# Edge stage: rows of local destinations as one-byte numbers, eight groups per transfer in two buffers

## The chip, the cores and the metric

The kernel runs on one core of one Trainium2 chip. The metric is the device time of one execution in microseconds (us), the median of several runs. TensorE is called PE, VectorE DVE, ScalarE ACT, GpSimd POOL and SyncE SP, as in the profile; PEld is PE's weight load, and SPq and POOLq are the sequencers of SP and POOL.

## What is computed

One graph attention layer over 6250 nodes and 206250 edges (100000 pairs in both directions and the self loops, sorted by destination), and behind it a mixture of 16 experts, of which each node uses two:

```
z  = layernorm(x) @ W                       # 4 heads of 64
e  = leaky_relu(es[src] + ed[dst], 0.01)    # es, ed: z against a_src, a_dst
ex = exp(e - max over the destination's edges)
x  = x + segment_sum(ex / denom[dst] * z[src], dst)
x  = x + moe(layernorm(x))                  # top 2 of 16 experts, layernorm behind it
```

The change is in the attention's edge part: for each edge the number of its destination within a tile of 128 nodes (the local destination, dst & 127) is wanted.

## The kernel before

The kernel has five stages. Stage A projects the nodes and writes a table of z with the source scores, 260 floats a row, to HBM (`z_table`). It also takes dst & 127 of all edges (L502), turns that into bf16 (L503, `dst_mod_h`) and stores it in HBM as one long row (`dst_rows`, L305). Stage B is the edge stage. Stages C, D and E route the nodes to experts, run these and combine their results.

Stage B works on 403 groups of 4 x 128 edges. A group whose edges belong to more than one tile of 128 destination nodes is visited once for each tile; the program has a fixed 451 visits, with tables (`visit_group`, `visit_word`, `group_free`) computed in stage A that say which group and tile a visit is. The loop is written out, and each engine has its own fixed order:

- POOL gathers. For each group it waits until the group four before it has been used (`group_free`, on `b_msg`) and issues four indirect DMAs (L681), each of 128 rows of `z_table`, into one of the four slots of `ring`. That makes 1612 gathers.
- SP relays. It waits for a group's four gathers and adds one to `b_group` (L629, `relay`), on which ACT waits. It also loads the local destinations: a transfer (L632) reads a piece of `dst_rows` and writes it to all 128 partitions of `dst_bc`, SP waits for its landing and adds one to `b_rows` (L643), on which DVE waits. A buffer is loaded again when DVE has made the last comparison on it (`b_ST`, L637 to L638 are that wait).
- DVE at step v: the sum of the scores for visit v - 5 (L747), the comparison ST (L734) for visit v, the leaky relu (L752), the accumulation of visit v - 8 (L835), the shift (L758), the comparison S (L740) for visit v - 6, the clamp (L765) and the message (L821) for visit v - 6, whose end frees the ring. ST compares the 512 local destinations of a group, the same in all partitions, with the partition's number (`iota_p`), and gives 128x512 floats, which are PE's weights for fetching destination scores (L927).
- PE at step v: four products (L927) for visit v and four (L938) for visit v - 6. All are f32 and are seen as eight weight loads and eight matmuls each.
- ACT: the copy of the source scores out of the ring (L866), the local destinations of L740 (L855) and the exponentials (L873, L875).

In the last 40 to 50 steps DVE, ACT and PE also finish the attention and normalise (L780 to L811, L885, L898, L950).

Before the change the transfer of L632 holds two groups (a pair) as bf16, in four buffers. SP's order for group g is: if g is even, wait for the landing of pair g/2 + 3 and tell DVE; wait for the landing of group g and tell ACT; if g is odd, wait for the comparison and issue the load of pair (g - 1)/2 + 4.

Of the kernel before, what the change touches and what calls it, by code (L numbers as in the profile page):

```python
# [27 lines left out]
F32 = mybir.dt.float32  # L28
I32 = mybir.dt.int32
BF16 = mybir.dt.bfloat16  # L30
ALU = mybir.AluOpType
ACT = mybir.ActivationFunctionType
AX = mybir.AxisListType

P = 128
G = 4
RING = 4
ROWS = 8
SLOPE = 0.01
EPS = 1e-5  # L40
LEVEL = 64.0
# [61 lines left out]
def early(item, depth):  # L103

    return isinstance(item, int) and item < depth


def gnn_moe_kernel(nc, E, x, x_turned, src_cols, dst_cols, dst_flat, dst_last, W, a_src, a_dst, gate_w, gate_b, w1, b1, w2, b2, gamma, beta, out):
    N, D = out.shape
    HEADS, DH = a_src.shape  # L110
    EXPERTS, _, F = w1.shape
    TOP = 2
    NT = -(-N // P)
# [5 lines left out]
    GROUPS = -(-CHUNKS // G)  # L119
# [4 lines left out]
    VISITS = FULL + NT  # L124
    BLOCKS = -(-CHUNKS // P)
# [4 lines left out]
    assert N * TOP // P > HEAD  # L130

    z_table = nc.dram_tensor("z_table", [NT * P, ROW], F32).ap()
    dst_rows = nc.dram_tensor("dst_rows", [BLOCKS * P * P], BF16).ap()
    norm_rows = nc.dram_tensor("norm_rows", [NT * P, D], F32).ap()

    pair_rows = nc.dram_tensor("pair_rows", [(TOP * NT + TILES) * P, D], F32).ap()
# [3 lines left out]
    def sem(name):  # L140
        return nc.alloc_semaphore(name=name)

    def sb(ctx, name, shape, dt=F32):
        return ctx.enter_context(nc.sbuf_tensor(name, shape, dt))
# [4 lines left out]
    def over(ap, shape):  # L149
        return ap.to_broadcast(shape)  # L150

    with whole:
# [32 lines left out]
        group_free = sb(graph, "group_free", [1, GROUPS + 1], I32)  # L185
# [5 lines left out]
        def bulk_rstd(step, stats, at, ready):  # L191

            a, b, m = ln_tmp[:, 0, at], ln_tmp[:, 1, at], mean[:, at]
            step(nc.vector.tensor_tensor(m, stats[:, at, 1], stats[:, at, 4], ALU.add))
            step(nc.vector.tensor_scalar(m, m, 0.5, None, ALU.mult))
            step(nc.vector.tensor_tensor(a, stats[:, at, 1], m, ALU.subtract))
            step(nc.vector.tensor_tensor(a, a, a, ALU.mult))
            step(nc.vector.tensor_tensor(b, stats[:, at, 2], stats[:, at, 5], ALU.add))
            nc.vector.scalar_tensor_tensor(out=a, in0=b, scalar=1.0 / D, in1=a, op0=ALU.mult, op1=ALU.add).then_inc(ready, 1)

# [31 lines left out]
        with ExitStack() as ctx:  # L232
# [1 line left out]
            dst_raw = sb(ctx, "dst_raw", [P, BLOCKS * P], I32)  # L234
            dst_i = sb(ctx, "dst_i", [P, BLOCKS * P], I32)
            dst_mod = sb(ctx, "dst_mod", [P, BLOCKS * P], I32)
            dst_mod_h = sb(ctx, "dst_mod_h", [P, BLOCKS * P], BF16)
            wcat = sb(ctx, "wcat", [P, KD, D + 2 * HEADS])
            centred = sb(ctx, "centred", [P, KD, D + 2 * HEADS])
            wprod = sb(ctx, "wprod", [P, 2, KD, D])  # L240
# [314 lines left out]
        b_over = sem("b_over"); b_go = sem("b_go")  # L555
        b_pstep = sem("b_pstep"); b_nodes = sem("b_nodes")
        b_group = sem("b_group")
        PAIRED, PAIRS = ROWS // 2, -(-GROUPS // 2)
        b_dst = [sem(f"b_dst{i}") for i in range(PAIRED)]; b_rows = sem("b_rows")
        b_S = sem("b_S"); b_ST = sem("b_ST")  # L560
        b_dest = sem("b_dest"); b_estep = sem("b_estep"); b_arg = sem("b_arg"); b_p = sem("b_p")
        b_msg = sem("b_msg"); b_sum = sem("b_sum"); b_acc = sem("b_acc"); b_es = sem("b_es")
# [28 lines left out]
        with ExitStack() as ctx:  # L591
# [6 lines left out]
            es_edge = sb(ctx, "es_edge", [P, 4, G, HEADS])  # L598
            S = sb(ctx, "S", [P, MR, G, P])
            ST = sb(ctx, "ST", [P, MR, G * P])  # L600
            dst_bc = sb(ctx, "dst_bc", [P, ROWS, G * P], BF16)
            earg = sb(ctx, "earg", [P, 4, 3, G * HEADS])
            msg = sb(ctx, "msg", [P, MR, G, ROW])
            psE = [ps(ctx, f"psEb{i}") for i in range(SR // BANKED)]
# [14 lines left out]
            @block.sync  # L619
            def _(sp):  # L620
                npass = sp.value_load(npass_i[0:1, 0:1], min_val=1, max_val=PASSES_MAX)
                with sp.Fori(0, npass) as k:
                    def uses(s):
                        return len(range(s, GROUPS, RING))

                    def relay(g, s, r):

                        sp.wait_ge(b_landed[s], 16 * G * (k * uses(s) + r + 1))
                        sp.nop().then_inc(b_group, 1)  # L629

                    def load_pair(g, at):
                        sp.dma_start(dst_bc[:, 2 * at:2 * at + 2, :].rearrange("p o f -> p (o f)"),  # L632
                                     over(dst_rows[bass.ds(g * (G * P), 2 * G * P)].unsqueeze(0), [P, 2 * G * P])).then_inc(b_dst[at], 16)

                    def replace_pair(g, at):

                        done = sp.value_load(group_free[0:1, g + 1 - ROWS + RING:g + 2 - ROWS + RING], min_val=1, max_val=VISITS)  # L637
                        sp.wait_ge(b_ST, done)  # L638
                        load_pair(g, at)

                    def relay_pair(at, r):
                        sp.wait_ge(b_dst[at], 16 * (r + 1))
                        sp.nop().then_inc(b_rows, 1)  # L643
                    for at in range(PAIRED):
                        load_pair(2 * at, at)
                    for at in range(PAIRED - 1):
                        relay_pair(at, 0)

                    for g in range(GROUPS):
                        pair = g // 2 + PAIRED - 1  # L650
                        if g % 2 == 0 and pair < PAIRS:
                            relay_pair(pair % PAIRED, pair // PAIRED)
                        relay(g, g % RING, g // RING)
                        if g % 2 and g // 2 + PAIRED < PAIRS:
                            replace_pair(g + ROWS - 1, g // 2 % PAIRED)

                    for at in range(PAIRED):
                        sp.wait_ge(b_dst[at], 16 * len(range(at, PAIRS, PAIRED)))
                    for done, total in ((b_group, GROUPS), (b_rows, PAIRS), (b_S, VISITS), (b_ST, VISITS), (b_dest, VISITS), (b_estep, 3 * VISITS),
                                        (b_arg, VISITS), (b_p, VISITS), (b_msg, VISITS + 1), (b_sum, VISITS), (b_acc, VISITS), (b_es, VISITS),  # L660
                                        (b_fstep, FIN_STEPS), (b_rden, NB), (b_scaled, NT), (b_added, NB), (b_stats, NT), (b_var, len(SPANS)),
                                        (b_root, len(SPANS)), (b_ready, len(SPANS)), (b_xn, NT), (b_xT_ps, NT), (b_xT, NT), (b_log_ps, NT), (b_log, NT),
                                        *((b_saved[i], 16 * len(range(i, NT, XN))) for i in range(XN)), (b_pstep, PASS_STEPS), (b_nodes, 1)):
                        sp.wait_ge(done, total)
                    sp.wait_ge(b_over, 4 * k + 4)
                    sp.sem_inc(apart, 1)
                    sp.sem_clear(range(b_pstep.num, b_saved[-1].num + 1))
                    sp.sem_inc(b_go, 1)
# [21 lines left out]
            def _(dve):  # L690
# [5 lines left out]
                with dve.Fori(0, npass) as k:  # L696
# [28 lines left out]
                    def make_ST(v, s, r):  # L725
                        if early(v, SOON):
                            group = dve.value_load(visit_group[0:1, v:v + 1], min_val=0, max_val=GROUPS - 1)
                        else:
                            group = (word[0] >> (RING * TILE_SPAN).bit_length() - 1).with_bounds(min_val=0, max_val=GROUPS - 1)
                        slot = group & (ROWS - 1)  # L730
                        dve.wait_ge(b_rows, (group >> 1) + 1)
                        if not early(v, MR):
                            dve.wait_ge(b_dest, v - MR + 1)
                        nc.vector.tensor_scalar(ST[:, s % MR, :], dst_bc[:, bass.ds(slot, 1), :].rearrange("p o f -> p (o f)"), iota_p[:, 0:1], None, ALU.is_equal).then_inc(b_ST, 1)  # L734
# [91 lines left out]
                    def accumulate(v, s, r):  # L826
# [5 lines left out]
                        if not early(v, 1):  # L832
                            dve.wait_ge(b_acc, v)
                        at = acc[:, bass.ds(tile, 1), :].rearrange("p o c -> p (o c)")
                        nc.vector.tensor_tensor(at, at, psM[s % 2][:, 0:ROW], ALU.add).then_inc(b_acc, 1)  # L835
                    written_out(VISITS, SR, [(look_up, AHEAD + 1), (e_add, AHEAD), (make_ST, 0), (e_lrelu, AHEAD),
                                                       (accumulate, AHEAD + 1 + MSG_TO_ACC), (e_shift, AHEAD), (one_hot, AHEAD + 1),
                                                       (e_clamp, AHEAD), (message, AHEAD + 1), (finish, None)], steps=FINISH)
# [134 lines left out]
        with ExitStack() as ctx:  # L973
# [6 lines left out]
            total = sb(ctx, "total", [P, EXPERTS, NT])  # L980
# [7 lines left out]
            slot_i = sb(ctx, "slot_i", [P, 3, NT], I32)  # L988
            iota_h = sb(ctx, "iota_h", [P, P], BF16)
            tile_h = sb(ctx, "tile_h", [P, NT], BF16)  # L990
            HALF = (NT + 1) // 2
            LR = 3
            THIRD = -(-NT // 3)
            low = sb(ctx, "low", [P, LR, THIRD, P], BF16)
            high = sb(ctx, "high", [P, LR, THIRD, 3, TILES], BF16)
# [469 lines left out]
```

## Time and profile before

| | us |
|---|---|
| median of 3 runs, without the profiler | 2771.41 |
| lowest and highest of them | 2768.65, 2774.7 |
| span of the profiled execution | 3426.8 |
| of it, ahead of the first gather of stage B | 79.36 |
| of it, from the first to the end of the last gather | 2724.53 |
| of it, behind that | 622.91 |

The profiled execution is 655 us longer than the median of the others. Engines' busy times are shares of its span: PE 68%, POOL 54%, DVE 49%, ACT 22%. Durations of single instructions can be read from it as they are; its waits must be read with care, for the reason the prediction gives.

### The profile page before, as it was taken

Reading aid. Unit: us, or ns where it says so; the run is one execution under the profiler, and the core shown is the slowest. Engines: PE = TensorE matmul, PEld = TensorE weight load, DVE = VectorE, ACT = ScalarE, POOL = GpSimd, SP = SyncE. Lnnn points to the kernel's source line nnn. Section 1 sums busy time; section 2 is a strip of 40 time slices with the busy share of each in tenths; the row PEclk is TensorE's granted clock in tenths of the full one; section 3 lists DMA queues with packets and bytes.
Section 4 is the critical chain, followed back from the end, with each engine's and each line's share of the span. In section 5 each row is a group of like instructions: output and inputs, shape, how many; then the busy total and the mean of one; then the engine's idle time right before and its main releaser. Section 6 shows DMA issues by size and latency. Waiting matters only on the chain. (4 is left out here: it accounts for less than half of the span.)

```text
span 3426.8 us, 54564 instructions
## 1 busy us (share of the span) xinstructions
PE 2313.2 (68%) x10829; PEld 1980.6 (58%) x10830; DVE 1684.5 (49%) x4860; ACT 753.9 (22%) x2906; POOL 1837.6 (54%) x1951
## 2 busy tenths in 40 slices
PE   6556666566667576666666665656567774899997
PEld 4545555455556565555555554545456662699995
DVE  6544445444455444454544454545456666533335
ACT  4111111111111111111111111111114442455556
POOL 1655555555555565555555555555555531555556
PEclk9677777776777666777777777777776775899999
DMA  8333333333334333333333333333334430563337
GB/s 285 97 102 96 105 92 99 98 103 93 101 101 105 97 106 100 97 100 103 97 100 97 103 101 105 94 100 97 100 99 109 111 88 21 184 185 105 106 104 234
DMA packets 183059, 378.55 MB, mean 110 GB/s; under 512 B 38773, under 2 KB 86816, under 8 KB 182410
## 3 DMA queue, kind: packets, MB, share of 16 engines
q0 software_dynamic: 87744, 243.02, 26.5%
q1 hardware_dynamic: 72152, 111.89, 10.4%
q10 hardware_dynamic: 22898, 20.85, 2.3%
q14 instruction: 189, 1.55, 0.2%
q8 instruction: 76, 1.25, 0.1%
HBM read 341.68 MB, written 33.93 MB: 110 GB/s over the span
## 5 line engine op out<-in xcount | busy, mean ns | idle before, releaser
L681 POOL DMA_INDIRECT ring<-z_table,src_idx x1612 | 1543.3, 957 | 1186.6 <-DVE msg L821 677.8
L938 PE MATMUL psMb<-msg,S 128*128 128x260 f32 x3608 | 1269.1, 512 | 515.1 <-DVE msg L821 413.0
L938 PEld LDWEIGHTS psMb<-msg,S 128*128 128x128 f32 x3608 | 878.7, 256 | 693.2 <-DVE msg L821 425.9
L927 PEld LDWEIGHTS psEb<-nodes,ST 128*128 128x128 f32 x3608 | 612.3, 241 | 515.5 <-issue 475.2
L927 PE MATMUL psEb<-nodes,ST 128*128 x3608 | 558.0, 279 | 451.3 <-DVE earg L765 183.2
L835 DVE TENSOR_TENSOR acc<-acc,psMb 128x260 f32 x451 | 190.3, 422 | 1080.3 <-remote 820.6
L821 DVE TENSOR_TENSOR msg<-ring,psPb 128x1024 f32<-128x1024 f32 x451 | 546.5, 1212 | 8.1 <-issue 8.1
L866 ACT COPY es_edge<-ring 128x16 f32 x451 | 91.8, 204 | 1128.5 <-issue 1045.0
L873 ACT ACTIVATE msg<-earg 128x16 f32<-128x16 f32 x451 | 95.2, 211 | 1064.9 <-DVE earg L765 927.3
L740 DVE TENSOR_TENSOR S<-iota_f,psPb 128x512 f32<-128x512 f32 x451 | 306.4, 679 | 2.7 <-issue 2.7
L734 DVE TENSOR_SCALAR ST<-dst_bc,iota_p 128x512 f32 x451 | 221.5, 491 | 53.7 <-issue 49.7
L1237 PE MATMUL psHd<-xT,w_sb 128*128 128x128 f32 x1728 | 213.2, 277 | 0.0
L1249 PE MATMUL psYd<-w_all,hid 128*128 x864 | 204.3, 380 | 1.7 <-ACT hid L1272 1.7
L1237 PEld LDWEIGHTS psHd<-xT,w_sb 128*128 128x128 f32 x1728 | 204.3, 194 | 0.1
L1205 POOL DMA_INDIRECT rows_sb<-norm_rows,src_sb x108 | 111.0, 1028 | 168.9 <-DVE src_sb L1282 151.5
L747 DVE TENSOR_TENSOR earg<-es_edge,psEb 128x16 f32<-128x16 f32 x451 | 73.8, 164 | 219.7 <-issue 105.1
L1293 DVE COPY xT<-psXd 128x256 f32<-128x256 f32 x108 | 45.8, 424 | 264.1 <-PE psXd L1227 257.9
L1249 PEld LDWEIGHTS psYd<-w_all,hid 128*128 128x128 f32 x864 | 156.0, 191 | 18.6 <-issue 1.9
L1260 ACT COPY w_sb<-w_all 128x1024 f32 x108 | 112.8, 1045 | 162.2 <-PE psHd L1237 85.6
L1212 POOL DMA_INDIRECT pair_rows<-y_sb,dst_sb x108 | 106.7, 988 | 45.6 <-issue 36.1
L1272 ACT ACTIVATE hid<-psHd,b1T 128x128 f32<-128x128 f32 x432 | 123.2, 368 | 30.9 <-issue 26.2
L855 ACT ACTIVATE psPb<-dst_col,visit_base 128x4 f32 x451 | 120.4, 267 | 42.4 <-DVE msg L821 20.5
(202 smaller groups left out, 1445.5 us busy)
## 6 DMA issues: line engine op xcount, KB each, us to landing
dst_bc<-dst_rows SPq DMA_DIRECT2D x202, 256.0 KB
ring<-z_table,src_idx POOLq DMA_INDIRECT x1612
w_all<-in_L_ffn_w_dram SPq DMA_DIRECT2D x32, 512.0 KB
b_sb<-in_L_ffn_b_dram ACTq DMA_DIRECT2D x108, 128.0 KB
got<-pair_rows SPq DMA_DIRECT2D x48, 256.0 KB, 4.5
z_table<-z_out SPq DMA_DIRECT2D x49, 130.0 KB, 7.1
norm_rows<-xnb ACTq DMA_DIRECT2D x49, 128.0 KB
acc<-in_x_turned_dram SPq DMA_DIRECT2D x12, 512.0 KB, 8.9
```

The costliest lines, as they stand in the source:

```text
L681: nc.gpsimd.indirect_dma_start(ring[:, s, c, :], None, z_table, bass.IndirectOffsetOnAxis(ap=at, axis=0)).then_inc(b_landed[s], 16)
L734: nc.vector.tensor_scalar(ST[:, s % MR, :], dst_bc[:, bass.ds(slot, 1), :].rearrange("p o f -> p (o f)"), iota_p[:, 0:1], None, ALU.is_equ ...
L740: nc.vector.tensor_tensor(S[:, s % MR, :, :], over(iota_f[:, 0:P].unsqueeze(1), [P, G, P]), over(psP[s % 2][:, G * HEADS:G * HEADS + G].un ...
L821: nc.vector.tensor_tensor(msg[:, s % MR, :, 0:D].rearrange("p g (h d) -> p g h d", h=HEADS), ring[:, bass.ds(slot, 1), :, 0:D].rearrange(" ...
L835: nc.vector.tensor_tensor(at, at, psM[s % 2][:, 0:ROW], ALU.add).then_inc(b_acc, 1)
L855: nc.scalar.activation(psP[s % 2][:, G * HEADS:G * HEADS + G], dst_col[:, bass.ds(group * G, G)], ACT.Identity, bias=visit_base[:, v:v + 1])
L927: last = nc.tensor.matmul(dest_of(s)[:, c * SH:(c + 1) * SH], ST[:, s % MR, c * P:(c + 1) * P], nodes[:, bass.ds(tile, 1), :].rearrange("p ...
L938: last = nc.tensor.matmul(psM[s % 2][:, 0:ROW], S[:, s % MR, c, :], msg[:, s % MR, c, :], start=c == 0, stop=c == G - 1)
L1237: last = nc.tensor.matmul(psH[s % 2][:, f * P:(f + 1) * P], w1_sb[:, s % 2, c, f * P:(f + 1) * P], xT[:, s % 2, c, :], start=c == 0, stop= ...
L1249: last = nc.tensor.matmul(psY[s % 2][:, 0:D], hid[:, s % 2, f, :], w2_f, start=f == 0, stop=f == FC - 1)
L1260: nc.scalar.copy(w1_sb[:, s % 2, :, :].rearrange("p c f -> p (c f)"), w_all[:, bass.ds(e, 1), 0:KD * F].rearrange("p o f -> p (o f)")).the ...
L1272: last = nc.scalar.activation(hid[:, s % 2, f, :], psH[s % 2][:, f * P:(f + 1) * P], ACT.Relu, bias=b1T[:, bass.ds(e, 1), f:f + 1].rearran ...
```

## The change

`dst_rows`, `dst_mod_h` and `dst_bc` become unsigned one-byte numbers in place of bf16. `dst_bc` holds 16 groups in place of 8, in the same number of bytes, as two buffers of eight groups. One transfer loads eight groups (4096 bytes to each partition) in place of two (2048 bytes). There are 51 transfers in place of 202. SP waits for the landing of part g // 8 + 1 ahead of group g with g % 8 = 2, three groups after the load was issued (behind group g with g % 8 = 7), where before it waited in the next group. DVE waits on `b_rows` with the group's number divided by 8. The comparison of L734 reads bytes.

```diff
-ROWS = 8
+ROWS = 16
+LOADED = 8
-    dst_rows = nc.dram_tensor("dst_rows", [BLOCKS * P * P], BF16).ap()
+    dst_rows = nc.dram_tensor("dst_rows", [BLOCKS * P * P], U8).ap()
-            dst_mod_h = sb(ctx, "dst_mod_h", [P, BLOCKS * P], BF16)
+            dst_mod_h = sb(ctx, "dst_mod_h", [P, BLOCKS * P], U8)
-            dst_bc = sb(ctx, "dst_bc", [P, ROWS, G * P], BF16)
+            dst_bc = sb(ctx, "dst_bc", [P, ROWS, G * P], U8)
-                    def load_pair(g, at):
-                        sp.dma_start(dst_bc[:, 2 * at:2 * at + 2, :].rearrange("p o f -> p (o f)"),
-                                     over(dst_rows[bass.ds(g * (G * P), 2 * G * P)].unsqueeze(0), [P, 2 * G * P])).then_inc(b_dst[at], 16)
+                    def load_rows_of(part, at):
+                        sp.dma_start(dst_bc[:, LOADED * at:LOADED * (at + 1), :].rearrange("p o f -> p (o f)"),
+                                     over(dst_rows[bass.ds(part * (LOADED * G * P), LOADED * G * P)].unsqueeze(0), [P, LOADED * G * P])).then_inc(b_dst[at], 16)
-                    for at in range(PAIRED):
-                        load_pair(2 * at, at)
-                    for at in range(PAIRED - 1):
-                        relay_pair(at, 0)
+                    for part in range(PARTED):
+                        load_rows_of(part, part)
+                    for part in range(PARTED):
+                        relay_rows_of(part)
                     for g in range(GROUPS):
-                        pair = g // 2 + PAIRED - 1
-                        if g % 2 == 0 and pair < PAIRS:
-                            relay_pair(pair % PAIRED, pair // PAIRED)
+                        part = (g + LOADED - 2) // LOADED
+                        if g % LOADED == 2 and PARTED <= part < PARTS:
+                            relay_rows_of(part)
                         relay(g, g % RING, g // RING)
-                        if g % 2 and g // 2 + PAIRED < PAIRS:
-                            replace_pair(g + ROWS - 1, g // 2 % PAIRED)
+                        if g % LOADED == LOADED - 1 and g // LOADED + PARTED < PARTS:
+                            replace_rows_of(g // LOADED + PARTED, g // LOADED % PARTED)
-                        dve.wait_ge(b_rows, (group >> 1) + 1)
+                        dve.wait_ge(b_rows, (group >> (LOADED.bit_length() - 1)) + 1)
```

## Rows read from the trace of the kernel before

**Rows 1.** The page: busy time by engine, and PE's granted clock in slices of 86 us.
```profile
PE 2313.2 (68%) x10829; PEld 1980.6 (58%) x10830; DVE 1684.5 (49%) x4860; ACT 753.9 (22%) x2906; POOL 1837.6 (54%) x1951
...
PEclk9677777776777666777777777777776775899999
```

**Rows 2.** Stretches: us; PE, PEld, DVE, ACT, POOL busy; PEclk; DMA share; GB/s.
```profile
0.00:79.36 79.36, 54.68 (x206) 41.11 (x207) 47.30 (x176) 38.51 (x105) 5.20 (x19) 0.99 0.87 294
79.36:2803.89 2724.53, 1729.87 (x7349) 1480.45 (x7350) 1362.89 (x3769) 393.41 (x2037) 1543.25 (x1612) 0.72 0.38 101
2803.89:3426.80 622.91, 528.64 (x3275) 459.08 (x3273) 274.26 (x917) 322.03 (x765) 289.11 (x320) 0.89 0.42 131
```

**Rows 3.** Lines: the gathers; count, busy us, mean ns, idle before and its releasers.
```profile
L681 POOL DMA_INDIRECT ring<-z_table,src_idx x1612 | 1543.3, 957 | 1186.6 <-DVE msg L821 677.8 <-issue 503.5 <-DVEq L696 5.3
```

**Rows 4.** Waits: engine, line, whom for, us in total, times, longest.
```profile
DVE acc L835 <- remote: 820.6, 112, 11.9
```

**Rows 5.** Timeline, start of the edge stage: start us, us, engine, line, operation.
```profile
79.36 1.44 POOL L681 DMA_INDIRECT ring<-z_table,src_idx  x1 [5.34 <-DVEq L696]
81.10 3.99 POOL L681 DMA_INDIRECT ring<-z_table,src_idx  x1 [0.30 <-issue]
92.05 3.03 POOL L681 DMA_INDIRECT ring<-z_table,src_idx  x1 [0.30 <-issue]
80.83 13.43 DVE L718 TENSOR_TENSOR acc<-acc,decided 128x3136 f32<-128x3136 f32 x4
```

**Rows 6.** Timeline: one comparison ST and the gather beside it.
```profile
286.95 0.49 DVE L734 TENSOR_SCALAR ST<-dst_bc,iota_p 128x512 f32 x1 [0.27 <-issue]
287.10 1.16 POOL L681 DMA_INDIRECT ring<-z_table,src_idx  x1 [0.30 <-issue]
```

**Rows 7.** Timeline of a stall and of the visits behind it.
```profile
1499.78 0.60 PE L938 MATMUL psMb<-msg,S 128*128 128x260 f32 x2
1510.10 0.42 DVE L835 TENSOR_TENSOR acc<-acc,psMb 128x260 f32 x1 [9.24 <-remote]
1512.41 0.48 DVE L734 TENSOR_SCALAR ST<-dst_bc,iota_p 128x512 f32 x1
1515.19 0.48 DVE L734 TENSOR_SCALAR ST<-dst_bc,iota_p 128x512 f32 x1
1516.09 1.71 PE L927 MATMUL psEb<-nodes,ST 128*128 x8
1517.66 3.58 PE L938 MATMUL psMb<-msg,S 128*128 128x260 f32 x8
1521.07 0.95 PE L927 MATMUL psEb<-nodes,ST 128*128 x8
1521.88 2.00 PE L938 MATMUL psMb<-msg,S 128*128 128x260 f32 x8
```

**Rows 8.** DMA queues from 300 to 2500 us: packets, MB, share of 16 engines; issues.
```profile
q0 software_dynamic: 62659, 173.84, 30.4%
q1 hardware_dynamic: 23475, 42.74, 6.5%
...
dst_bc<-dst_rows SPq DMA_DIRECT2D x163, 256.0 KB
```

**Rows 9.** Waits of SP's queue.
```profile
SPq L643 <- DMA dst_bc<-dst_rows: 150.2, 56, 3.4
SPq L309 <- DMA dst_rows<-dst_mod_h: 1.5, 1, 1.5
```

**Rows 10.** Lines of DVE by shape: count, busy us, mean ns, idle before.
```profile
L821 DVE TENSOR_TENSOR msg<-ring,psPb 128x1024 f32<-128x1024 f32 x451 | 546.5, 1212 | 8.1 <-issue 8.1
L740 DVE TENSOR_TENSOR S<-iota_f,psPb 128x512 f32<-128x512 f32 x451 | 306.4, 679 | 2.7 <-issue 2.7
L503 DVE CAST dst_mod_h<-dst_mod 128x1664 bf16<-128x1664 int32 x1 | 1.0, 1026 | 0.0
```

**Rows 11.** The tile ring: shortest, median and longest gather, ns.
```profile
L681 POOL DMA_INDIRECT ring<-z_table,src_idx x1612: 940/946/3989, 79.4 to 2802.9; - x180
```

More of the change, by code:

```diff
@@ L30 @@
 BF16 = mybir.dt.bfloat16
+U8 = mybir.dt.uint8
 ALU = mybir.AluOpType
@@ L557, in gnn_moe_kernel @@
         b_group = sem("b_group")
-        PAIRED, PAIRS = ROWS // 2, -(-GROUPS // 2)
-        b_dst = [sem(f"b_dst{i}") for i in range(PAIRED)]; b_rows = sem("b_rows")
+        PARTED, PARTS = ROWS // LOADED, -(-GROUPS // LOADED)
+        assert PARTS * LOADED * G <= BLOCKS * P
+        b_dst = [sem(f"b_dst{i}") for i in range(PARTED)]; b_rows = sem("b_rows")
         b_S = sem("b_S"); b_ST = sem("b_ST")
@@ L629, in relay @@
                         sp.nop().then_inc(b_group, 1)
-                    def load_pair(g, at):
-                        sp.dma_start(dst_bc[:, 2 * at:2 * at + 2, :].rearrange("p o f -> p (o f)"),
-                                     over(dst_rows[bass.ds(g * (G * P), 2 * G * P)].unsqueeze(0), [P, 2 * G * P])).then_inc(b_dst[at], 16)
-                    def replace_pair(g, at):
-                        done = sp.value_load(group_free[0:1, g + 1 - ROWS + RING:g + 2 - ROWS + RING], min_val=1, max_val=VISITS)
+                    def load_rows_of(part, at):
+                        sp.dma_start(dst_bc[:, LOADED * at:LOADED * (at + 1), :].rearrange("p o f -> p (o f)"),
+                                     over(dst_rows[bass.ds(part * (LOADED * G * P), LOADED * G * P)].unsqueeze(0), [P, LOADED * G * P])).then_inc(b_dst[at], 16)
@@ L638, in replace_pair, with replace_rows_of, relay_rows_of @@
+                    def replace_rows_of(part, at):
+                        freed = (part - PARTED + 1) * LOADED - 1 + RING
+                        done = sp.value_load(group_free[0:1, freed:freed + 1], min_val=1, max_val=VISITS)
                         sp.wait_ge(b_ST, done)
-                        load_pair(g, at)
-                    def relay_pair(at, r):
-                        sp.wait_ge(b_dst[at], 16 * (r + 1))
+                        load_rows_of(part, at)
+                    def relay_rows_of(part):
+                        sp.wait_ge(b_dst[part % PARTED], 16 * (part // PARTED + 1))
@@ L653, in _ @@
                         relay(g, g % RING, g // RING)
-                        if g % 2 and g // 2 + PAIRED < PAIRS:
-                            replace_pair(g + ROWS - 1, g // 2 % PAIRED)
-                    for at in range(PAIRED):
-                        sp.wait_ge(b_dst[at], 16 * len(range(at, PAIRS, PAIRED)))
-                    for done, total in ((b_group, GROUPS), (b_rows, PAIRS), (b_S, VISITS), (b_ST, VISITS), (b_dest, VISITS), (b_estep, 3 * VISITS),
+                        if g % LOADED == LOADED - 1 and g // LOADED + PARTED < PARTS:
+                            replace_rows_of(g // LOADED + PARTED, g // LOADED % PARTED)
@@ L660, in _ @@
+                    for at in range(PARTED):
+                        sp.wait_ge(b_dst[at], 16 * len(range(at, PARTS, PARTED)))
+                    for done, total in ((b_group, GROUPS), (b_rows, PARTS), (b_S, VISITS), (b_ST, VISITS), (b_dest, VISITS), (b_estep, 3 * VISITS),
                                         (b_arg, VISITS), (b_p, VISITS), (b_msg, VISITS + 1), (b_sum, VISITS), (b_acc, VISITS), (b_es, VISITS),
```

## The prediction
> **What bounds the kernel now.** I read the page first. POOL is busy 54% of the span and PE 68%, and the granted clock of PE is 0.6 to 0.7 in the slices of the edge stage against 0.9 at both ends [rows 1]. No engine looks full, so the next view is the three stretches around the gathers: 79.36 us ahead of the first, 2724.53 us with them, 622.91 us behind the last [rows 2]. Only the middle one holds what the change touches, apart from one conversion and one store.
>
> In the middle stretch the gathers are the plainest clockwork. 1612 of them take 957 ns each, and POOL is idle 1186.6 us before them [rows 3]. That idle time has two parts: 503.5 us of "issue" and 677.8 us of waiting for a message of DVE [rows 3]. Single gathers show what most of the first part is: 0.30 us before each [rows 5, 6]. So a gather that waits for nothing costs 0.957 + 0.30 = 1.257 us, and all of them 1543.3 + 1612 x 0.30 = 1543.3 + 483.6 = **2026.9 us**. What is left of the stretch, 2724.5 - 2026.9 = 697.6 us, is POOL waiting for the ring.
>
> Now the profiled execution against the runs. It spans 3426.8 us where the median is 2771.4. Take the same head and tail: 2771.4 - 79.4 - 622.9 = 2069.1 us would be left for the gathers, 42 us above their own 2026.9. So without the profiler nearly all of the 697.6 us of waiting is gone, and POOL's issuing sets the stage's pace: 2069.1 / 451 visits = 4.6 us a visit. (If something lies around the span in the median, the 42 shrink by it.) What the waits of the profiled execution are is seen in the largest group of DVE: 820.6 us before the accumulation, 112 times, put down to no engine here [rows 4]. One such place: PE's last product of the visit ends at 1500.38, and the accumulation that wants it starts at 1510.10 [rows 7]. Every engine then stands, and the ring runs dry. That is a disturbance the timed runs don't pay, at least not at this size; I take no gain or loss from it.
>
> How far the others are from POOL's 4.6 us a visit: DVE, when nothing holds it, starts its comparisons 2.78 us apart (1512.41 and 1515.19). PE needs 0.95 + 2.00 = 2.95 us a visit at the upper clock, but 1.71 + 3.58 = 5.29 us at the lower [rows 7]. Stretches at the lower clock, and the last 40 to 50 steps where DVE, PE and ACT have more to do, are my guess for the 42 us.
>
> **The change part by part.**
>
> *The transfers.* 202 of 256 KB become 51 of 512 KB (4096 bytes to each of 128 partitions), so the bytes written fall from 53 to 27 MB. From 300 to 2500 us SP's queue takes 6.5% of the 16 engines, POOL's 30.4% [rows 8]: 36.9% together, so the engines are not the bound, and halving 6.5% frees about 3% of something with 60% to spare. Price: 0. Cover: the ring. It lets POOL run four groups ahead, so a landing may come late by what the loop leaves: three groups of 5.03 us (15.1 us) from the end of a group's gathers until its slot is wanted again, less the landing, SP's and ACT's relay, and two steps of DVE (2 x 2.78) with a message of 1.2 us. With 2 us for the landing that is about 15.1 - 2 - 0.5 - 5.6 - 1.2 = 5.8 us of slack. The landing time and the relay are my estimates, from the transfers' longest wait of 3.4 us [rows 9] as an upper end of the landing.
>
> *The larger burst.* It puts 128 packets of 4096 bytes in front of a gather's packets where there were 128 of 2048. Now 6.5% of 2200 us is 143 us on each engine for 163 transfers, 0.9 us each [rows 8]. If the time grows with the bytes, a burst takes 1.8 us on each engine where it took 0.9. Bounds for the extra delay of a gather in front of which it falls: 0 and 0.9 us, below the 5.8 us of slack. Price 0; the upper bound without that cover is 51 x 0.9 = 46 us.
>
> *SP's order.* Before, SP stood 150.2 us for landings of pairs, 56 times, at most 3.4 us [rows 9], right ahead of the relay of a group. A group lands 5.03 us after the one before, so a wait of 3.4 us behind one relay ends before the next is due; it hid nothing and delayed nothing. After the change the landing is asked for only three groups (15 us) after the load and the wait is nothing. The waits on the comparison stay satisfied: when group g has landed, DVE has sent the message of group g - 4, and it compares six visits ahead of its messages. Saved on SP: 150 us, 151 issues and 151 waits; on the path: 0. Bounds: 0 and, if each of the 202 waits had held a relay and the ring had no slack, the 42 us that POOL waits at all.
>
> *DVE's wait on the rows.* It now asks for whole parts of eight groups. The part of groups 8m + 8 and up is told ahead of the relay of group 8m + 2, and DVE reaches the comparison of group 8m + 8 only behind the sum for 8m + 3 or later, which needs a later relay. So this wait is never last. At the start two transfers of 512 KB stand in for four of 256 KB (three of them waited for). DVE's first comparison comes behind 13.43 us of L718, which end at 94.26 us [rows 5], and this hides a few us. Price 0.
>
> *The comparison on bytes.* L734 takes 0.48 to 0.49 us for 512 elements [rows 6, 7]. Two-source operations show the plain rate: (1212 - 679) / 512 = 1.04 ns an element [rows 10], by which 512 elements alone are 533 ns, more than all of L734. So L734 runs in a faster mode, about twice the plain rate. So does the conversion of int32 to bf16: 1664 elements in 1.03 us, 1.73 at the plain rate [rows 10]. Widths of four and two bytes are thus seen in this mode; one byte is not. I take the same duration (nearest rows), price 0. The other end is the plain rate: 0.48 + 256 x 1.04 ns = 0.75 us, 0.27 us more a visit, 120 us of DVE time in all, hidden by 4.6 - 2.8 = 1.8 us a visit of DVE's slack, except at the end of the stage.
>
> At the other end there would also be a gain. A gather that starts 0.15 us after such a comparison takes 1.16 us [rows 6] where the median is 0.946 [rows 11]; another takes 3.03 us beside L718 [rows 5]. The mean of 957 ns is 11 above the median of 946 [rows 3, 11]: 1612 x 0.011 = 17.7 us, of which the first five (1.44, 3.99 and three of about 3.03, [rows 5]) are 14.5 - 5 x 0.95 = 9.8 too long. So about **8 us** go to the comparisons, and would come back if L734 left the fast mode.
>
> The Trainium skill (SBUF — State Buffer, "Who interferes with whom") says the same of the cause: VectorE in a two-port mode and GpSimd exclude each other from a shared pair of ports for a whole instruction. The Trainium skill (Vector Engine (DVE) Microarchitecture Reference, 5.1 Performance modes) gives this mode's conditions without a width of the elements; by that rule the bytes keep the mode and the sum stays at 0, and no row here has a one-byte operand to test it. The Trainium skill (DMA: Bandwidth & Descriptors, Rules for kernel authors) asks for transfers of 1 MiB and more. By it the change is a gain for DMA time; what it would be here is 0, since the share of 6.5% [rows 8] binds nothing.
>
> *Stage A.* The conversion writes bytes (1.0 us, or 1.0 more at the plain rate, beside the projection) and the store is half as large. SP waits 1.5 us for it [rows 9], at the end of the stage; half the bytes might give 0.2 us. Price 0, bounds -0.3 and +1.
>
> **Sum.** Against the profiled execution: 0 of 3426.8 us. Against the median: 2771.4 + 0 = **2771 us**.
>
> **The rivals.**
>
> *The bytes drop the comparison to the plain rate, and POOL gains.* For it: no one-byte operand is in the trace. Against it: four and two bytes behave alike. It gives 2771 - 8 = 2763 us.
>
> *The relays held the ring.* SP's 150 us in front of relays mattered in the undisturbed execution too, or lighter DMA traffic speeds landings. Against it: 3.4 us at most within 5 us. It can take from the 42 us only; a third of them gives 2771 - 14 = 2757 us.
>
> *Slower: the plain rate meets the end of the stage.* In the last 49 visits DVE also finishes the attention. If DVE is the bound there, each visit grows by 0.27 us, 13 us in all, less 1 us that POOL gets back there. That gives 2783 us. It decides once the comparison is longer and DVE is the last to be ready; if the comparison on bytes took over 0.48 + 1.8 = 2.3 us it would decide in every visit. The larger burst in a place without slack would end in the same range (up to 46 us, and a third of that is 15).
>
> *The change does not do what it says* (DMA splits rows of 4096 bytes otherwise, or reads the same bytes of HBM more slowly): it ends where the forecast does, since SP has 15 us for the landing.
>
> **How the numbers follow.** No change, within 0.2% (5.5 us, about what a measurement of this kernel can tell from none): 0.60. The first rival 0.12 and the second 0.11, both faster; the third and the burst 0.17, slower. The forecast's own range is 2766 to 2777. For 8 in 10 the range reaches into both sides: below through 2757 to 2750, above through 2783 to 2788.
>
> **What would show it.** Right: L734 at 0.48 us, gathers still 0.95 + 0.30 us apart, 26 MB less on SP's queue, and L643's wait near 0, with the runs unchanged. Wrong: L734 near 0.75 us (first or third rival, told apart by the sum of POOL's idle time behind 2560 us); a mean gather below 0.95 us; or waits for rows before L734. What would make the whole prediction wrong is a wrong reading of the 655 us: if the stalls were partly paid in the timed runs, the ring would have no slack there, and landings, relays and DVE's order would all count.

## The result, and the profile after

| | before | after |
|---|---|---|
| median of 12 runs, us | 2776.37 | 2786.62 |
| lowest, us | 2768.65 | 2783.12 |
| ratio, 95% interval | | 1.0039 (1.0029 to 1.0049) |

The change makes the kernel 0.4% slower, some 10 us. The forecast was no change, 2771 us. One of the 12 runs of the kernel before took 2913.96 us and is not in the ratio. Of the 15 us between the forecast and the measured 2786.62, 5 us are the kernel before itself, whose median was 2771.41 with 3 runs and is 2776.37 with 12.

The trace ahead of the prediction, 3426.8 us long, does not belong to the times beside it. Experiments e3 to e6 met a chip on which every kernel took 3409 to 3461 us, with or without the profiler (but for one run of 3684.97), and their traces show the stalls of [rows 4, 7]. So the first trace was very likely taken on a chip of that sort; its chip is not on record, and only one such chip was met, so a lasting property of it can't be told from a passing state. The changed kernel's trace is of the usual sort. So it is set beside a second trace of the kernel before (run e0 below), not beside [rows 2, 3].

The page of the changed kernel (first lines and granted clock) and its three stretches, with the columns of [rows 2]:

```profile
span 2783.2 us, 53814 instructions
PE 2253.5 (81%) x10829; PEld 1873.0 (67%) x10830; DVE 1709.0 (61%) x4860; ACT 720.6 (26%) x2906; POOL 1859.3 (67%) x1951
...
PEclk9676888788787877888688788888777669999998
```
```profile
0.00:79.30 79.30, 55.22 (x206) 41.52 (x207) 47.21 (x176) 38.55 (x105) 5.20 (x20) 0.93 0.86 292
79.30:2167.15 2087.85, 1675.41 (x7362) 1378.26 (x7363) 1388.46 (x3776) 361.93 (x2047) 1566.12 (x1612) 0.80 0.43 119
2167.15:2783.20 616.05, 522.85 (x3263) 453.18 (x3261) 273.31 (x911) 320.13 (x755) 287.98 (x320) 0.90 0.42 132
```

Its groups of gathers and of the comparison ST, which answer to [rows 3] and to L734 in [rows 6, 7]:

```profile
L685 POOL DMA_INDIRECT ring<-z_table,src_idx x1612 | 1566.1, 972 | 526.7 <-issue 444.7 <-DVE msg L825 77.0 <-DVEq L700 5.0
L738 DVE TENSOR_SCALAR ST<-dst_bc,iota_p 128x512 f32 x451 | 230.0, 510 | 98.0 <-issue 93.4 <-PE psEb L931 4.3
```

And SP's waits in the edge stage, its queue from 300 to 1900 us and its transfers, which answer to [rows 8, 9]:

```profile
SPq L632 <- DMA ring<-z_table,src_idx: 1994.3, 401, 11.6
SPq L647 <- DMA dst_bc<-dst_rows: 4.3, 2, 3.2
```
```profile
q1 hardware_dynamic: 5616, 20.45, 3.4%
...
dst_bc<-dst_rows SPq DMA_DIRECT2D x39, 512.0 KB, 4.0
```

The reader is to see that the change did on SP and on the DMA engines what it says. SP waits 4.3 us for rows, and its queue takes 3.4%. DVE's comparison is no longer than before. Yet the gathers take 972 ns each, where [rows 3] has 957 and the second trace of the kernel before, shown next, has 965.

### The profile page after: what moved, and what is told of

Its sections match the earlier page's. It is cut to its first block and busy times, and to the rows that moved or that the text cites. A ratio compares the mean times of both kernels' runs of the same rounds, so it can differ in the third digit from the quotient of the medians.

```text
span 2783.2 us, 53814 instructions
## 1 busy us (share of the span) xinstructions
PE 2253.5 (81%) x10829; PEld 1873.0 (67%) x10830; DVE 1709.0 (61%) x4860; ACT 720.6 (26%) x2906; POOL 1859.3 (67%) x1951
## 5 line engine op out<-in xcount | busy, mean ns | idle before, releaser
L685 POOL DMA_INDIRECT ring<-z_table,src_idx x1612 | 1566.1, 972 | 526.7 <-issue 444.7
L942 PE MATMUL psMb<-msg,S 128*128 128x260 f32 x3608 | 1199.2, 490 | 169.5 <-DVE msg L825 168.2
L942 PEld LDWEIGHTS psMb<-msg,S 128*128 128x128 f32 x3608 | 827.4, 241 | 334.2 <-DVE msg L825 186.6
L931 PEld LDWEIGHTS psEb<-nodes,ST 128*128 128x128 f32 x3608 | 548.9, 226 | 346.3 <-issue 323.3
L931 PE MATMUL psEb<-nodes,ST 128*128 x3608 | 535.1, 276 | 219.4 <-DVE ST L738 111.5
L738 DVE TENSOR_SCALAR ST<-dst_bc,iota_p 128x512 f32 x451 | 230.0, 510 | 98.0 <-issue 93.4
```

Source lines behind the costliest of these rows:

```text
L685: nc.gpsimd.indirect_dma_start(ring[:, s, c, :], None, z_table, bass.IndirectOffsetOnAxis(ap=at, axis=0)).then_inc(b_landed[s], 16)
L931: last = nc.tensor.matmul(dest_of(s)[:, c * SH:(c + 1) * SH], ST[:, s % MR, c * P:(c + 1) * P], nodes[:, bass.ds(tile, 1), :].rearrange("p ...
L942: last = nc.tensor.matmul(psM[s % 2][:, 0:ROW], S[:, s % MR, c, :], msg[:, s % MR, c, :], start=c == 0, stop=c == G - 1)
```

## The experiments

**The kernel before once more**, for a trace of the usual sort of chip; no edit.

> The kernel before, unchanged, for a trace without the stalls of the first. The changed kernel's trace has, from the first to the last gather, 2087.8 us: 1612 gathers at 0.946 + 0.305 us, 9.8 us of slow gathers at the start, 31 us because 138 later gathers take 1.1 to 1.2 us beside a comparison (L738), and 31 us of waits for the ring from group 374 on. Theory A (the collisions decide): this trace has the same end and fewer collisions, some 10 us less of them and fewer than 100 long gathers. Theory B (the end decides): the same collisions, 31 us, and about 20 us of waits at the end in place of 31. Theory C (the start or the tail): both sums equal, and the difference lies before 79 us or behind the last gather.

Its profiled run took 2773.76 us. Stretches, gathers, comparison and SP's waits:

```profile
0.00:79.06 79.06, 54.39 (x206) 41.01 (x207) 47.33 (x176) 38.56 (x105) 5.20 (x20) 0.98 0.88 295
79.06:2154.95 2075.89, 1671.83 (x7353) 1378.36 (x7354) 1388.88 (x3772) 361.48 (x2045) 1555.58 (x1612) 0.80 0.49 132
2154.95:2771.80 616.85, 524.69 (x3271) 455.95 (x3269) 273.93 (x913) 320.71 (x757) 288.12 (x320) 0.90 0.41 132
```
```profile
L681 POOL DMA_INDIRECT ring<-z_table,src_idx x1612 | 1555.6, 965 | 526.0 <-issue 453.9 <-DVE msg L821 66.4 <-DVEq L696 5.7
L734 DVE TENSOR_SCALAR ST<-dst_bc,iota_p 128x512 f32 x451 | 231.5, 513 | 99.0 <-issue 96.6 <-PE psEb L927 1.9 <-SPq L643 0.3
```
```profile
SPq L629 <- DMA ring<-z_table,src_idx: 1216.5, 403, 11.7
SPq L643 <- DMA dst_bc<-dst_rows: 623.7, 197, 4.4
```

The head and the tail are the same within 1 us. The middle stretch is 2087.85 - 2075.89 = 12.0 us longer after the change. POOL's own time is 1566.1 - 1555.6 = 10.5 us of that, its idle time 0.7 us. So the loss is in the duration of gathers, as theory A of the expectation above has it (its count of fewer than 100 long gathers was missed by one). From the starts and durations of all gathers (the first five left out, which stand beside L718 in both; a pause of POOL is 0.305 us where nothing is waited for, and a wait is what lies above that):

```
                                    before   after
gathers over 1.0 us                    100     138
what gathers take over 0.946 us, us   20.9    31.4
waits of POOL over 0.35 us, us        29.5    31.0
```

Where the long ones are, the timeline of the changed kernel shows (POOL, the copy of the scores on ACT, the comparison on DVE):

```profile
1116.48 0.20 ACT L870 COPY es_edge<-ring 128x16 f32 x1 [4.15 <-SPq L632]
1117.16 0.49 DVE L738 TENSOR_SCALAR ST<-dst_bc,iota_p 128x512 f32 x1 [0.27 <-issue]
1117.27 1.19 POOL L685 DMA_INDIRECT ring<-z_table,src_idx  x1 [0.30 <-issue]
...
1126.97 0.20 ACT L870 COPY es_edge<-ring 128x16 f32 x1 [4.69 <-SPq L632]
1127.65 0.53 DVE L738 TENSOR_SCALAR ST<-dst_bc,iota_p 128x512 f32 x1 [0.27 <-issue]
1127.72 0.95 POOL L685 DMA_INDIRECT ring<-z_table,src_idx  x1 [0.30 <-issue]
```

The comparison follows the copy by 0.68 us each time. At 1117 it starts 0.11 us ahead of a gather, and the gather takes 1.19 us. At 1127 it starts 0.07 us ahead, and the gather takes 0.95. Over the comparisons of both traces that start up to 0.40 us ahead of a gather:

```
ahead of the gather by, us   0-0.05  0.05-0.10  0.10-0.15  0.15-0.20  0.20-0.25  0.25-0.30  0.30-0.35  0.35-0.40
before: times                    34         95         42         11          3         15          3          5
before: gather longer by, us   0.00       0.02       0.24       0.19       0.12       0.09       0.04       0.00
after: times                     30        132         75         17          5          6          5          8
after: gather longer by, us    0.00       0.04       0.24       0.19       0.12       0.09       0.03       0.00
```

The cost of a collision is the same for bf16 and for bytes. What differs is how often the comparison falls into the window of 0.10 to 0.35 us: 74 times before, 108 times after. Gathers with a comparison that started up to 0.5 us ahead of them lose 16.0 us before and 27.2 us after, 11.2 us more; all others lose 4.9 and 4.3. So this one sort of collision is the whole difference of 10.5 us.

The comparison falls into the window by a rhythm. POOL starts a gather every 1.251 us. A group lands some 3.0 us behind the start of its fourth gather when nothing holds it up (in the changed kernel half of the odd groups reach ACT between 2.97 and 3.03 us behind it). SP, ACT and DVE pass that on in a fixed time. So the comparison meets the third gather of the next group at nearly the same distance, 0.07 us ahead in the median of these groups, just short of the window. A group that lands late misses the third gather. In the kernel before, that is so for most of the even groups, whose gathers are in flight beside the pair's transfer that SP issues one group earlier. An odd group, the late even group behind it, and the next odd group:

```profile
1110.64 0.20 ACT L866 COPY es_edge<-ring 128x16 f32 x1 [4.22 <-SPq L629]
1111.08 10.65 SPq L632 DMA_DIRECT2D dst_bc<-dst_rows  x2
1111.33 0.49 DVE L734 TENSOR_SCALAR ST<-dst_bc,iota_p 128x512 f32 x1 [0.28 <-issue]
1111.49 1.15 POOL L681 DMA_INDIRECT ring<-z_table,src_idx  x1 [0.30 <-issue]
...
1117.23 0.20 ACT L866 COPY es_edge<-ring 128x16 f32 x1 [5.99 <-SPq L629]
1117.91 0.49 DVE L734 TENSOR_SCALAR ST<-dst_bc,iota_p 128x512 f32 x1 [0.28 <-issue]
1117.94 0.95 POOL L681 DMA_INDIRECT ring<-z_table,src_idx  x1 [0.30 <-issue]
...
1120.99 0.20 ACT L866 COPY es_edge<-ring 128x16 f32 x1 [3.16 <-SPq L629]
1121.67 0.49 DVE L734 TENSOR_SCALAR ST<-dst_bc,iota_p 128x512 f32 x1 [0.28 <-issue]
1121.69 0.95 POOL L681 DMA_INDIRECT ring<-z_table,src_idx  x1 [0.30 <-issue]
```

The row of L632 holds two issues, at 1111.08 and 10.3 us later. The copy at 1110.64 is 2.9 us behind its group's fourth gather, and the comparison behind it strikes a third gather (1111.49). The copy at 1117.23 is 4.3 us behind its own; its comparison comes only when the third gather is over, starts 0.03 us ahead of the fourth and costs it nothing. SP's own wait for the pair is not what comes late here: it ended 0.36 us or more, in the median 1.21 us, ahead of each even group's relay.

By the same reckoning over groups 16 to 369 (median time from the start of a group's fourth gather to the copy on ACT, and how often the third gather of the next group took over 1.0 us):

```
                         even groups          odd groups
before                   3.30 us, 12 times    3.00 us, 37 times
bytes, pairs (e1)        3.05 us, 31 times    3.00 us, 37 times
after                    3.02 us, 50 times    2.99 us, 48 times
after + copies (e8)      3.59 us,  4 times    3.01 us, 54 times
```

**Theory A** in full: the change takes away the transfers that made every second group land 0.3 us late, and with them an accident that kept its comparison off the gather. The later runs test that. It covers the even groups, 38 of the 49 third gathers that the change adds. The odd groups add 11 with no change in their landing that the table can show; their comparison starts 0.06 us ahead of the gather before and 0.07 us after, close to the window's edge, and why those 11 were added stays open.

**Bytes alone**: U8 for `dst_rows`, `dst_mod_h` and `dst_bc`, and nothing else.

```diff
-    dst_rows = nc.dram_tensor("dst_rows", [BLOCKS * P * P], BF16).ap()
+    dst_rows = nc.dram_tensor("dst_rows", [BLOCKS * P * P], U8).ap()
```

> Bytes alone: the row is stored and compared as one-byte numbers, still two groups to a transfer in four buffers, with the order of SP as before. If the bytes make the loss (the comparison's hold on POOL, or its own length), the ratio to the kernel before is 1.004, as for the whole change. If the loss comes from eight groups to a transfer and from SP's new order, it is 1.000.

Measured: 1.0022 (1.0012 to 1.0033), between the two. A pair of bytes has half the bytes of a pair of bf16, and its even groups land 0.05 us late in place of 0.30 (table). In its one trace the long gathers sum to 21.7 us, only 0.8 more than before, and its profiled run (2776.96 us) is the second fastest of its 11; the ratio is the better witness. So by the ratios the loss comes in about two halves, with the bytes and with the eight groups. That the first half also comes by late landings is a reading of the table (31 third gathers in place of 12), not shown apart.

**Larger transfers alone**: bf16, ROWS = 8, LOADED = 4, SP's wait moved to the next group.

```diff
-                        part = (g + LOADED - 2) // LOADED
-                        if g % LOADED == 2 and PARTED <= part < PARTS:
+                        part = g // LOADED + 1
+                        if g % LOADED == 0 and PARTED <= part < PARTS:
```

> Larger transfers alone: bf16 as before, four groups to a transfer in two buffers, so that each transfer writes 4096 bytes to each partition as in the change, and there are 101 of them. SP waits for the landing in the next group, as before. If the burst of 512 KB is the cause, twice as many of them as in the change give a ratio of 1.004 to 1.008. If the bytes are the cause, it is 1.000. If it is that SP hardly waits between relays, it lies between 1.000 and 1.004, as SP here waits for every fourth group in place of every second.

Measured: 1.0059 (1.0043 to 1.0075), in the range that was expected if the burst of 512 KB is the cause. It doesn't tell that, for another cost came in. Two buffers of four groups leave no time between the last comparison on one and the first on the next, and DVE waits for the rows, a wait that neither the kernel before nor the changed one has:

```profile
DVE ST L738 <- SPq L647: 164.9, 48, 4.7
```

Its edge stage is 2090.5 us, 14.6 more than in e0. Of that POOL's waits are 11.3 us (40.8 in place of 29.5), its gathers 3.2. So most of its loss is waiting that the changed kernel (31.0 us of waits) doesn't have. A cost of the larger burst is bounded by e7 and e10 below, not by this run.

**The comparison one place later, idle copies on HBM, idle copies on ACT**: all on a chip where the kernel before took 3428.72 us (median of 23 runs).

```diff
-  [(look_up, AHEAD + 1), (e_add, AHEAD), (make_ST, 0), (e_lrelu, AHEAD),     # e3 (after), e4 (before)
+  [(look_up, AHEAD + 1), (e_add, AHEAD), (e_lrelu, AHEAD), (make_ST, 0),
```
```diff
+                        if g % 2 == 0 and g:                                  # e5
+                            sp.wait_ge(b_dst[PARTED], 16 * (g // 2))
                         relay(g, g % RING, g // RING)
+                        if g % 2 and g < GROUPS - 1:
+                            sp.dma_start(idle[g // 2 % 2, :, :],
+                                         over(dst_rows[bass.ds(2048 * (g % 64), 2048)].unsqueeze(0), [P, 2048])).then_inc(b_dst[PARTED], 16)
```
```diff
+                        for i in range(2):                                    # e6
+                            nc.scalar.copy(late[:, s % 4, i, :], ring[:, bass.ds(slot, 1), 0, 0:16].rearrange("p o c -> p (o c)"))
                         nc.scalar.copy(es_edge[:, s % 4, :, :],
```

> The changed kernel with DVE's comparison ST one place later in the visit, behind the leaky relu (L756 before L738); nothing is left out. In the trace of the changed kernel the comparison starts 0.88 us behind the relay of a group and so 0.1 to 0.2 us ahead of the third gather of the next group, which then takes 1.1 to 1.2 us. Theory A (the loss is these collisions): it now starts some 0.3 us later, just behind the gather's start; the 138 long gathers fall below 50, 15 to 30 us are saved, and the time is 2755 to 2770 us, below both kernels (ratio to before 0.993 to 0.999). Rival (the large transfers delay landings): nothing about them is changed, and the ratio stays at 1.004.

> The kernel before with the same move of the comparison behind the leaky relu. Theory A: its 80 or so collisions (20.8 us) go too, and it ends within 3 us of the changed kernel with the move, since nothing else of the change counts: ratio 0.993 to 0.999. Rival: if bytes and eight groups to a transfer cost time by themselves, this one stays 8 to 12 us below the changed kernel with the move.

> The changed kernel with extra work: behind every second group SP also copies 2048 bytes 128 times from HBM to HBM, into an array that nobody reads, and waits for it in the next group, as the kernel before did with its pairs. Theory A (the pairs' transfers made every second group land 0.3 us later, and so its comparison missed the gather): even groups land some 0.2 to 0.4 us later again, collisions fall from 31 to about 20 us, and the kernel with more work is 4 to 12 us faster than the changed one: ratio to before 0.999 to 1.002. Rival (DMA traffic costs time): it is slower than the changed kernel, ratio 1.004 to 1.010.

> The changed kernel with two copies of 16 elements on ACT, read by nobody, ahead of the copy of the source scores (L870), so that DVE's step starts some 0.2 to 0.3 us later behind each relay. Theory A: a longer path to DVE makes it faster, for the comparison starts behind the gather's start: collisions below 15 us, ratio to before 0.995 to 1.000. Rival (what counts is how soon DVE gets its scores): the delay can only cost, ratio 1.004 or more.

Measured: e3 1.0071 (1.0048 to 1.0094), e4 1.0085 (1.0058 to 1.0112), e5 1.0019 (0.9994 to 1.0043), e6 1.0007 (0.9983 to 1.0031). Of what theory A forecast, the ratios of e3, e4 and e6 were missed; the ratio of e5 lies in its range, with an interval that reaches up to the rival's, and the collisions of e6 fell below 15 us as forecast. The changed kernel was not run on this chip, and the first trace, of such a chip, has only 8.5 us of long gathers, so there was little to gain. The waits of e6:

```profile
DVE acc L840 <- remote: 801.7, 114, 11.7
POOL ring L686 <- DVE msg L826: 702.0, 172, 9.2
```

These are the stalls of [rows 4] and [rows 3], in a kernel whose timed runs took 3430 us. What e6 saves on gathers (3.7 us against the first trace) POOL stands idle longer (5.1 us).

The losses of e3 and e4 are collisions too. The gathers of e3:

```profile
L685 POOL DMA_INDIRECT ring<-z_table,src_idx x1612 | 1564.9, 971 | 1188.6 <-DVE msg L825 733.1 <-issue 450.5 <-DVEq L700 5.0
```

Its long gathers take 30.2 us and those of e4 31.1, where the first trace has 8.5; the idle time of POOL is within 3 us of that of [rows 3], and the stage is 24.0 and 20.4 us longer than there. Some 17.7 and 17.5 us of it are in gathers that end a wait for the ring. In the first trace the last comparison starts 0.79 us ahead of such a gather in the median, outside the window; one place later it starts 0.23 us ahead, inside it (137 and 130 times). So the same move that was to take the comparison out of the window put it in at another gather.

The idle copies of e6 did shift the comparison: where no stall comes between, it starts 1.08 us behind SP's relay in place of 0.88, and the long gathers are 4.9 us. Three of the kernels were run once more on another chip.

**The same on a chip of the usual sort** (before: 2776.8 us, 15 runs), with the kernel before under the idle copies of e6 as the fourth.

> The same kernel as e6_after_scores_late (two idle copies on ACT ahead of L870), since on the chip of that call every kernel, the one before too, took 3430 us, and POOL waited 693 us for the ring whatever the comparison did. Its trace there had the comparison 1.08 us behind the relay in place of 0.88, and 4.8 us of collisions in place of 31. On a chip where the kernel before takes some 2775 us, theory A says 31 - 5 = 26 us less than the changed kernel: ratio to before 0.994 (0.991 to 0.998). Rival (a later step of DVE costs as much as it saves): 1.002 to 1.006.

> The same kernel as e5_after_idle_copies, again for a chip where the kernel before takes some 2775 us. Theory A (a transfer behind every second group makes the next land late and its comparison miss the gather): even groups are relayed 3.0 us or more behind their fourth gather in place of 2.8, their collisions fall to a third, and the kernel with more work is faster than the changed one: ratio to before 0.999 to 1.002. Rival (DMA traffic costs time): 1.004 to 1.010.

> The same kernel as e3_after_later_compare, for a chip where the kernel before takes some 2775 us. The comparison came 1.09 us behind the relay there, as with the idle copies. Theory A: the same gain as with the idle copies, ratio 0.994 (0.991 to 0.998), without extra work. Rival: 1.004.

> The kernel before with the same two idle copies on ACT. Theory A, if collisions are all that tells the two kernels apart: it gains what it has of them in its own trace (20.8 us) less 5, and ends at ratio 0.994 as the changed kernel with the copies does, within 0.001. Rival (bytes or large transfers cost or save time of their own): the two differ by 0.002 or more.

```
                                          ratio to before (95%)      long gathers, us   edge stage, us
e7   after, two idle copies on ACT        0.9952 (0.9938 to 0.9965)        9.9              2063.5
e9   after, comparison one place later    0.9961 (0.9946 to 0.9976)       14.1              2067.9
e10  before, two idle copies on ACT       0.9959 (0.9946 to 0.9973)       13.6              2069.9
e8   after, idle copies on HBM            1.0009 (0.9996 to 1.0021)       30.4              2091.0
     after (first result)                 1.0039 (1.0029 to 1.0049)       31.4              2087.8
```

Long gathers and edge stage are of the one trace of each. The changed kernel's own ratio is from the first comparison, on other runs of the kernel before (median 2776.37); it was not run again beside e7 to e10.

The gathers of e7, and one of its groups:

```profile
L686 POOL DMA_INDIRECT ring<-z_table,src_idx x1612 | 1544.6, 958 | 524.0 <-issue 465.8 <-DVE msg L826 53.1 <-DVEq L701 5.1
```
```profile
1105.78 0.31 ACT L872 COPY late<-ring 128x16 f32 x2 [4.00 <-SPq L633]
1106.18 0.20 ACT L873 COPY es_edge<-ring 128x16 f32 x1
1106.55 0.94 POOL L686 DMA_INDIRECT ring<-z_table,src_idx  x1 [0.30 <-issue]
1106.87 0.49 DVE L739 TENSOR_SCALAR ST<-dst_bc,iota_p 128x512 f32 x1 [0.27 <-issue]
```

Work that nobody reads, put on the path to DVE, takes the changed kernel from 1.0039 to 0.9952, 24 us, inside theory A's range. The comparison now starts behind the gather's start, and 21.5 of 31.4 us of long gathers are gone; the stage is 24.3 us shorter. The move of the comparison (e9) gives nearly the same with no extra work. With the idle copies the kernel before (e10) and the changed one (e7) differ by 0.0007, inside both intervals: once collisions are few, bytes and eight groups cost and save nothing that can be measured. Nothing here supports a cost of theirs apart from the rhythm. The expectation of e10 was met in that difference and missed in size: 0.9959 in place of 0.994, with 13.6 us of long gathers left in place of 5.

e8 is the reverse test: it adds 201 copies of 256 KB to the changed kernel, in the place where the pairs' transfers were, twice the 51 transfers' bytes. Its ratio is 1.0009, some 8 us below the changed kernel, in theory A's range and below the rival's. Its even groups strike a third gather 4 times in place of 50. But its profiled run was the slowest of its 11 (2786.3 us against a median of 2778.2), with more collisions of first gathers (28 in place of 14) and a median gather of 949 ns in place of 946, so its sum of 30.4 us and its stage of 2091.0 us don't show the gain that the median does. The link from late landings to the time thus rests on the ratio and on the even groups' count, not on a trace that adds up.

## Why the prediction was wrong

*POOL's issuing sets the pace*: right. The middle stretch was put at 2069.1 us and is 2075.9, 49.0 us above the 2026.9 of gathers and pauses. What I called 42 us of waiting is 29.5 us of waits, nearly all from group 374 on, 12.3 us of longer gathers (1555.6 in place of 1543.3) and 7 us of pauses, which are 0.305 us and not 0.30.

*The 655 us are a disturbance that the timed runs don't pay*: right for the runs shown, wrong in the cause. I took the profiler for it; on the chip of e3 to e6 the timed runs pay it too.

*The transfers, SP's order, DVE's wait on the rows, stage A*, each at 0: as far as the ring and SP are concerned, right. SP's waiting for rows fell from 623.7 to 4.3 us (I had 150.2 from the other chip [rows 9]), 26.4 MB left its queue, POOL's long waits went from 29.5 to 31.0 us, and head and tail stayed.

*The comparison on bytes*, same duration: right, 510 ns against 513, and 487 against 487 in the median. Neither rival that needed the plain rate came about.

*About 8 us go to the comparisons*: this is the term that was mis-sized, and the step that failed. The first trace had the mechanism in two rows, [rows 6], but POOL stood 690 us there in waits, and each stall broke the rhythm. Undisturbed the term is 20.9 us. And I let it stand as a constant of the kernel, that could only come back if L734 left the fast mode. It depends on where in POOL's rhythm the comparison starts, and 31.4 us is its value after the change: 10.5 us that the sum put at nothing, of the 12.0 us by which the stage grew.

*The larger burst* was weighed against the ring's slack of 5.8 us, and there it is nothing. I had written the size of the present transfer, 0.9 us, and not asked what the 0.3 us do by which it delays a landing, where that landing bounds nothing. The loss comes with the absence of that delay.

The third rival had the sign and nearly the size (2783 us), by a mechanism that the trace refutes: no longer comparison, no longer end of the stage. The measured time lies in the range, for a reason that no rival named.

## What to carry to other kernels

Where two engines shut each other out for part of an instruction and both run on a fixed rhythm, the cost is a matter of phase. A change that only takes away jitter can bring them into step. Before giving such a cost a constant, set the start of each of the one against the start of the next of the other and look for a window; then move the instruction by one place in its own order, which is the cheapest test. Count the collisions again behind the move: with the same move the changed kernel is 0.4% below the kernel before on one chip (e9) and 0.7% above it on another (e3), where the gathers start by another rhythm. And ask whether a trace's span fits the times beside it before reading waits or rates from it.

## What the runs showed of the hardware that I had not expected

- Gather and comparison hold each other up, each for a part of itself (3608 comparisons in the traces of after, e0 to e2 and e7 to e10). Alone a gather takes 0.946 us and a comparison 0.486.
  - A gather that starts 0.10 us behind the comparison's start takes 0.25 us more. The loss falls with the distance, to nothing at 0.35 us; the comparison keeps its 0.486 us.
  - A gather that starts less than 0.06 us behind it loses nothing (at most 0.005 us, 262 times). The comparison is the one that grows, to 0.519 us.
  - Between 0.06 and 0.10 us it is one or the other, never both: 80 times the gather takes 0.25 to 0.29 us more and the comparison 0.49 at most; 384 times the gather loses at most 0.011 us and the comparison takes 0.52 to 0.56.
  - A comparison that starts 0.45 to 0.70 us behind a gather's start takes up to 0.73 us. One that starts 0.35 to 0.45 us behind it makes the gather longer, by up to 0.11 us. One that starts earlier than that behind it costs neither of them anything, though the gather runs on.

  The Trainium skill (SBUF — State Buffer, "Who interferes with whom") says that whoever issues first has the shared pair of ports for the whole instruction and the other is fully blocked. The traces agree that one of the two waits for the other, and that either can be the loser. They don't show a hold for the whole instruction: a gather 0.11 us behind the comparison's start loses 0.24 us where 0.38 us of the comparison are left. When in a gather and in a comparison the ports are wanted is not shown directly.
- A one-byte source keeps the comparison's speed: 510 ns a time against 513 with bf16, f32 output in both. Some 25 ns of both means come from the comparisons that a gather held up; the medians are 487 and 487.
- The kernel before took 2776.37 us in the first comparison, 3428.72 us beside e3 to e6 and 2776.8 us beside e7 to e10. In the traces at 3430 us DVE waits some 800 us for sums of PE that by the record were computed some 9 us earlier [rows 7]; in the traces of 2760 to 2787 us it waits 42 to 69 us for PE there, and the views have no wait for "remote". What holds them back stays open.
